# A selective-scan block with a gated feed-forward network: scan tiles of 8 states x 16 channels instead of 1 state x 128 channels

## What is computed

```
xz = x @ W_in.T;  x_ssm, z = split(xz)                     # 256 channels each
x_ssm = silu(causal_conv(x_ssm, conv_w, 4 taps) + conv_b)  # per channel, over time
proj = x_ssm @ W_x.T                                       # 16 columns B, 16 columns C, 1 for dt
dt = softplus(proj[..., -1:] * W_dt + b_dt)                # 256 channels
A = -exp(A_log)                                            # 256 channels x 16 states
h[t] = exp(dt[t] * A) * h[t-1] + (x_ssm[t] * dt[t]) * B[t] # 256 x 16 states, over 256 steps
y[t] = sum over states of h[t] * C[t]
out  = ((y + x_ssm * D) * silu(z)) @ W_out.T
```

## Time and profile before

| what | value |
|---|---|
| median of 3 runs | 1126.44 us |
| profiled execution | 1125.33 us |
| its span in the trace | 1123.5 us |
| instructions | 14735 |
| granted TensorE clock, mean | 0.969 of full |
| DMA traffic | 152.28 MB, mean 136 GB/s |
| VectorE idle before it starts the first U product | until 20.65 us |

### The profile page before, as it was taken

One profiled execution on the slowest core, in us unless ns is written; L12 is line 12 of the kernel. 1 busy time (PEld: TensorE's weight loads), 2 busy tenths in 40 slices (PEclk: granted clock), 3 DMA queues, 4 the chain that ended last, 5 costly groups with the idle time before them and its releaser, 6 DMA issues.

```text
span 1123.5 us, 14735 instructions
## 1 busy us (share of the span) xinstructions
PE 1028.0 (92%) x4928; PEld 649.0 (58%) x4928; DVE 1029.9 (92%) x1484; ACT 901.6 (80%) x1257; POOL 854.8 (76%) x499
## 2 busy tenths in 40 slices
PE   4656999999999999999999999999999999998997
PEld 1435566575756556565656657575665757555543
DVE  4999999999999999999999999999999999999511
ACT  7664988989798988979898898989889897987231
POOL 1677878878797888869788887978788797888540
PEclk8686999999999999999999999999999999999999
DMA  4762340705325070622507061340707043060000
GB/s 179 274 240 80 128 184 10 320 11 200 132 79 242 12 319 11 253 78 92 230 21 310 11 266 65 143 188 15 306 10 306 25 180 141 31 291 1 19 10 10
DMA packets 44060, 152.28 MB, mean 136 GB/s; under 512 B 4560, under 2 KB 24016, under 8 KB 27728
## 3 DMA queue, kind: packets, MB, share of 16 engines
q1 hardware_dynamic: 43600, 151.02, 34.1%
q10 hardware_dynamic: 384, 0.32, 0.1%
HBM read 146.08 MB, written 5.24 MB: 135 GB/s over the span
## 4 chain that ended last, share of the span: by engine, by line
PE 69%; ACT 16%; DVE 7%; issue 6%; POOL 2%; DMA 0%; ACTq 0%; DVEq 0%; POOLq 0%
PE G L705 33%; PE Y L690 14%; ACT dA L335 6%; PE G L727 4%; PE G L712 3%; ACT g L378 3%; DVE hb L598 3%; PE G L673 2%; PE Y L653 2%; PE Y L735 2%; PE G L657 2%; DVE U L591 2%; PE G L709 1%; ACT L351 1%; ACT xs L351 1%
## 5 line engine op out<-in xcount | busy, mean ns | idle before, releaser
L320 POOL TENSOR_TENSOR pb<-hb,cbc 128x1024 f32<-128x1024 f32 x256 | 602.9, 2363 | 179.9 <-DVE hb L598 139.6
L598 DVE TENSOR_TENSOR_SCAN hb<-dA,U 128x512 f32<-128x512 f32 x512 | 594.8, 1205 | 0.0
L335 ACT ACTIVATE dA<-dt,negA 128x510 f32<-128x510 f32 x512 | 342.2, 712 | 62.3 <-DVE hb L598 60.8
L591 DVE TENSOR_TENSOR U<-X,bbc 128x512 f32<-128x512 f32 x512 | 327.0, 686 | 7.2 <-ACT X L341 6.4
L690 PEld LDWEIGHTS Y<-ident,pb 128*128 128x128 f32 x2048 | 244.1, 145 | 111.0 <-issue 73.0
L690 PE MATMUL Y<-ident,pb 128*128 128x128 f32 x2048 | 272.1, 280 | 31.9 <-POOL pb L320 31.9
L705 PE MATMUL G<-hid,h_sb 128*128 128x512 f32 x512 | 232.6, 598 | 1.0 <-ACT g L494 0.8
L705 PE MATMUL G<-g,h_sb 128*128 128x512 f32 x512 | 229.8, 593 | 0.0
L705 PEld LDWEIGHTS G<-hid,h_sb 128*128 128x128 f32 x512 | 96.0, 193 | 110.5 <-issue 107.7
L705 PEld LDWEIGHTS G<-g,h_sb 128*128 128x128 f32 x512 | 92.6, 190 | 94.5 <-issue 90.3
L310 POOL TENSOR_TENSOR hid<-hid,g 128x512 f32<-128x512 f32 x64 | 80.1, 1273 | 7.8 <-ACT g L494 7.8
(11 more groups left out here) (91 smaller groups left out, 997.7 us busy)
## 6 DMA issues: line engine op xcount, KB each, us to landing
cbc<-scr SPq DMA_DIRECT2D x64, 1024.0 KB, 7.8
bbc<-scr SPq DMA_DIRECT2D x63, 1024.0 KB, 9.1
xT_sb<-xT_d SPq DMA_DIRECT2D x16, 256.0 KB, 2.7
xtok_sb<-xtok_d SPq DMA_DIRECT2D x16, 256.0 KB, 2.9
out_d<-r SPq DMA_DIRECT2D x16, 256.0 KB, 2.4
h_sb<-h_d SPq DMA_DIRECT2D x2, 1024.0 KB, 22.3
bbc<-scr SPq DMA_DIRECT2D x2, 512.0 KB, 4.6
scr<-rows SPq DMA_DIRECT2D x62, 16.0 KB, 1.5
```

The lines of the kernel that those rows point to most:

```text
L320: nc.gpsimd.tensor_tensor(pb[:, qs:qs + 2, :], hb[:, hs:hs + 2, :], cbc[:, n:n + 2, :], ALU.mult).then_inc(s_p, 1)
L335: nc.scalar.activation(halves(dA[:, u % DA_RING, :])[:, :, 1:SEQ], halves(dt[:, par, c, :])[:, :, 1:SEQ], ACT.Exp, scale=negA[:, c, n:n + ...
L591: nc.vector.tensor_tensor(U[i][:], X[:], bbc[:, n + i, :], ALU.mult).then_inc(s_u, 1)
L598: nc.vector.tensor_tensor_scan(hb[:, 2 * (v % H_PAIRS) + i, :], dA[:, u % DA_RING, :], U[i][:], 0.0, ALU.mult, ALU.add).then_inc(s_h, 1)
```

## The change

A tile becomes 8 states x 16 channels (partition 16 s + d). B and C, repeated 16 times, then serve all tiles with the same 8 states, and dt and dt*x have to be spread over the 8 states of a tile. What is done:

- dt and dt*x of a block are stored to DRAM (`store_steps`, 4 transfers of 256 KB a block) and read back so that each of 16 channels' rows goes to 8 partitions (`spread_steps`, 1 MB each, for 4 tiles; 8 a block), into 3 slots each. Each load serves two groups of 4 tiles, one for each half of the states.
- B and C are spread by 2 transfers of 256 KB each a block (`spread_B`, `spread_C`). ScalarE copies B, not dt*x, into the PSUM bank X, three times a block instead of twice.
- TensorE sums the states of 4 tiles with 4 products of 128 x 32 selecting weights, each at another 32-column position of the array, with 512 tokens moving (`sum_group`). The sum has channels on the partitions. It is begun by a product with diag(D). The turn, its copy and ScalarE's scaling by D go; z is made with channels on the partitions too.
- The convolution of channels 128 to 255 is four products with weights w_in * tap, accumulated at shifted tokens (`in_conv`); ScalarE copies the result (`copy_conv`). The other half stays on VectorE.
- Orders move: ScalarE's silu of the convolution to step 1 (with an activation table load more), the softplus to steps 7 and 8, one half after the other; the output projection to step 2; the second residual sum to step 6; GpSimd's sum of dt and product to steps 9, 11 and 12 and the second norm to 13; the start too.

The diff, cut to its core:

```diff
+SN, SD = 8, 16
+NG = NS // SN
+GT = 4
+GROUPS = NG * DI // SD // GT
+TILES = GROUPS * GT
+PARITIES = 2
+LOADS = NC * PARITIES
+SLOTS = 3
+def states_of(k):
+    return (0, 0, 1, 1, 1, 1, 0, 0)[k]
...
-        bbc = sb("bbc", [P, NS, TB])
-        cbc = sb("cbc", [P, NS, TB])
+        brep = sb("brep", [P, NG, TB])
+        crep = sb("crep", [P, 2, NG, TB])
+        dtr = sb("dtr", [P, SLOTS, GT, TB])
+        xdr = sb("xdr", [P, SLOTS, GT, TB])
...
+            def spread_B(b, g):
+                if b > 0:
+                    sp.wait_ge(s_X, 3 * b - g)
+                piece = scr_rows[b % 2, g * SN:(g + 1) * SN, :]
+                sp.dma_start(brep[:, g, :], piece.unsqueeze(1).to_broadcast([SN, SD, TB])).then_inc(s_b[g], 16)
+            def store_steps(b, c, scr, x, s_stored):
+                to = scr[b % 2, c].rearrange("e d q t -> q (e d) t")
+                sp.dma_start(to, x[:, c, :]).then_inc(s_stored[c], 16)
+            def spread_steps(b, c, e, scr, o, s_o):
+                slot = group_no(b, c, e) % SLOTS
+                piece = scr[b % 2, c, e].rearrange("d q t -> d (q t)")
+                sp.dma_start(flat(o[:, slot, :, :]), piece.unsqueeze(0).to_broadcast([SN, SD, GT * TB])).then_inc(s_o[slot], 16)
...
+                if scan and j > 0:
                     sp.wait_ge(s_u, TILES * j)
+                    spread_steps(j, 1, 0, scr_xd, xdr, s_xdr)
+                if scan:
+                    sp.wait_ge(s_dA, TILES * j + 3 * GT)
+                    spread_steps(j, 1, 1, scr_dt, dtr, s_dtr)
...
+                if scan:
+                    sp.wait_ge(s_u, TILES * j + 3 * GT)
+                    spread_steps(j, 1, 1, scr_xd, xdr, s_xdr)
+                if front:
+                    sp.wait_ge(s_rows, A + 1)
+                    store_rows(A, range(NT))
+                    sp.wait_ge(s_dt, 2 * A + 1)
+                    store_steps(A, 0, scr_dt, dts, s_dts)
+                    sp.wait_ge(s_xd, 2 * A + 1)
+                    store_steps(A, 0, scr_xd, xds, s_xds)
+                if front:
+                    sp.wait_ge(s_dts[0], 16 * (A + 1))
+                    sp.wait_ge(s_dA, TILES * j + 4 * GT)
+                    spread_steps(A, 0, 0, scr_dt, dtr, s_dtr)
+                    sp.wait_ge(s_dt, 2 * A + 2)
+                    store_steps(A, 1, scr_dt, dts, s_dts)
+                    sp.wait_ge(s_xds[0], 16 * (A + 1))
+                    sp.wait_ge(s_u, TILES * j + 4 * GT)
+                    spread_steps(A, 0, 0, scr_xd, xdr, s_xdr)
+                    sp.wait_ge(s_xd, 2 * A + 2)
+                    store_steps(A, 1, scr_xd, xds, s_xds)
+                    sp.wait_ge(s_store, 16 * NT * (A + 1))
+                    spread_B(A, 0)
+                    spread_C(A, (0,))
+                if front:
+                    sp.wait_ge(s_dA, TILES * j + 7 * GT)
+                    spread_steps(A, 0, 1, scr_dt, dtr, s_dtr)
+                    sp.wait_ge(s_u, TILES * j + 7 * GT)
+                    spread_steps(A, 0, 1, scr_xd, xdr, s_xdr)
+                    spread_B(A, 1)
+                    spread_C(A, (1,))
...
+            def fill_X(b, i):
+                g = i % 2
+                if i < 2:
+                    act.wait_ge(s_b[g], 16 * (b + 1))
+                if b > 0 or i > 0:
+                    act.wait_ge(s_u, TILES * b + (0, 2 * GT, 6 * GT)[i])
+                nc.scalar.activation(X[:], brep[:, g, :], ACT.Copy).then_inc(s_X, 1)
...
-                            nc.vector.tensor_tensor(U[i][:], X[:], bbc[:, n + i, :], ALU.mult).then_inc(s_u, 1)
+                            nc.vector.tensor_tensor(U[i][:], X[:], xdr[:, slot, q + i, :], ALU.mult).then_inc(s_u, 1)
...
+            def in_conv(b):
+                for s in range(TAPS):
+                    last = nc.tensor.matmul(halves(bank_c1(b))[:, :, s:SEQ], wc1[:, TAPS - 1 - s, :],
+                                            halves(xT_sb[:])[:, :, 0:SEQ - s], start=(s == 0), stop=(s == TAPS - 1),
+                                            skip_group_check=True)
+                last.then_inc(s_c1, 1)
...
+            def start_sum(b, c):
+                if b > 0:
+                    pe.wait_ge(s_gate, 2 * b - 1 + c)
+                pe.wait_ge(s_xs, 2 * b + 1 + c)
+                nc.tensor.matmul(Y[c][:], diagD[:, c, :], xs[:, b % 2, c, :], start=True, stop=False,
+                                 skip_group_check=True).then_inc(s_start, 1)
+            def sum_group(b, k):
+                c, e, _ = load_of(k)
+                pe.wait_ge(s_p, STEPS * b + 2 * k + 2)
+                for q in range(GT):
+                    rows32 = slice(q * 2 * SD, (q + 1) * 2 * SD)
+                    last = nc.tensor.matmul(Y[c][rows32, :], sel_sb[:, e, :], pb[:, (GT * k + q) % (2 * P_PAIRS), :],
+                                            start=False, stop=(k % (GROUPS // NC) == GROUPS // NC - 1),
+                                            skip_group_check=True, tile_position=(0, q * 2 * SD))
                 last.then_inc(s_y, 1)
```

More of the change, by code:

```diff
@@ L447, in _, with run @@
-            decay(0, 0, 1, True)
-            softplus_part(1, ACT.Relu)
-            decay(0, 0, 2, True)
-            decay(0, 0, 3, True)
-            times_D(0, 0, 0)
-            softplus_rest(1)
-            for u in range(4, AHEAD):
-                decay(0, 0, u, True)
-            def run(j, par, scan, intake, front, back, tail):
-                first = isinstance(j, int) and j == 0
+            for u in range(AHEAD):
+                decay(0, u)
+            def run(j, scan, intake, front, back, tail):
@@ L572, in _ @@
-            nc.vector.tensor_tensor(X[:], dt[:, 0, 0, :], xs[:, 0, 0, :], ALU.mult).then_inc(s_xdt, 1)
-            def run(j, par, scan, intake, front, back, tail):
-                first = isinstance(j, int) and j == 0
+            nc.vector.tensor_tensor(dts[:, 0, :], dts[:, 0, :], soft[:, 0, :], ALU.add).then_inc(s_dt, 1)
+            dve.wait_ge(s_dt, 1)
+            dve.wait_ge(s_xs, 2)
+            nc.vector.tensor_tensor(xds[:, 0, :], dts[:, 0, :], xs[:, 0, 0, :], ALU.mult).then_inc(s_xd, 1)
@@ L651, in _ @@
         def _(pe):
-            def in_proj(b, c):
-                nc.tensor.matmul(bank_in(b, c), win_sb[:, c * P:(c + 1) * P], xT_sb[:], start=True, stop=True).then_inc(s_ip, 1)
-            def z_proj(b, i):
-                for t in range(2):
-                    last = nc.tensor.matmul(BZ[i][:, t * DI:(t + 1) * DI], tile_of(xT_sb, 2 * i + t), win_sb[:, DI:2 * DI],
-                                            start=(t == 0), stop=True, skip_group_check=True)
-                last.then_inc(s_z, 1)
@@ L661, in rows_proj, with in_proj @@
-            def rows_proj(b, par):
-                for c in range(NC):
-                    pe.wait_ge(s_xs, 2 * b + 1 + c)
+            def in_proj(b):
+                nc.tensor.matmul(bank_in(b), win_sb[:, 0:P], xT_sb[:], start=True, stop=True).then_inc(s_ip, 1)
+            def in_conv(b):
[4 more added lines that the diff above has]
+                last.then_inc(s_c1, 1)
@@ L674, in dt_proj @@
                 last.then_inc(s_dtb, 1)
-            def start_sum(b, par, c):
-                if not (isinstance(b, int) and b == 0):
-                    pe.wait_ge(s_gy, 2 * b - 1 + c)
-                pe.wait_ge(s_xD, 2 * b + c + 1)
-                for t in range(NT):
-                    last = nc.tensor.matmul(Y[c][:, t, :], tile_of(xD[:], t), ident[:], is_transpose=True,
-                                            start=(t == 0), stop=False, skip_group_check=True)
-                last.then_inc(s_start, 1)
@@ L746, in _ @@
             pe.wait_ge(s_xT, 16)
-            for c in range(NC):
-                in_proj(0, c)
+            in_proj(0)
+            pe.wait_ge(s_wc1, 1)
+            in_conv(0)
+            pe.wait_ge(s_wx, 16)
+            rows_proj(0)
+            dt_proj(0)
+            pe.wait_ge(s_pre0, 4)
             z_proj(0, 0)
@@ L751, in _, with run @@
             z_proj(0, 1)
-            pe.wait_ge(s_wx, 16)
-            pe.wait_ge(s_tap, 6)
-            rows_proj(0, 0)
-            pe.wait_ge(s_zc, 2)
-            dt_proj(0, 0)
             pe.wait_ge(s_ident, 16)
-            def run(j, par, scan, intake, front, back, tail):
-                first = isinstance(j, int) and j == 0
+            pe.wait_ge(s_diag, NC)
+            pe.wait_ge(s_sel, 16)
+            def run(j, scan, intake, front, back, tail):
                 I, A, F, T = j + 2, j + 1, j - 1, j - 2
-                if isinstance(j, int) and j == 1:
+                if j == 1:
@@ L777, in run @@
-                    if v >= LAG and scan:
-                        sum_pair(j, v - LAG)
-                    if v == 0 and first:
-                        pe.wait_ge(s_xT, 16 * 2)
-                        in_proj(1, 0)
-                    if v == 0 and tail and not (isinstance(j, int) and j == NB):
+                    if v == 1 and back:
+                        sum_group(F, GROUPS - 1)
```

(14 more changed lines are left out.)

645 lines of the change are left out of this document (311 added, 334 removed).

## The result

The changed kernel takes **1490.3 us** (median of 4 runs, 1488.0 to 1500.1) beside 1125.9 us of the kernel before on the same chip: a ratio of 1.326, 95% interval 1.319 to 1.332. The forecast was 1093 us with a range of 1081 to 1150. The change made the kernel a third slower.

The account below looks back on a forecast made before the run. VectorE was taken to set the 64.60 us block, TensorE 1.5 behind: 1125.3 - 33.3 (taps) - 5.4 (residual wait) + 9 (start) - 6.5 (end) - 1.4 (turn, copy) = 1087.7, plus 4 for tight places and 1.1 to the median: 1093 us, range 1081 to 1150.

Parts of the forecast that it names:

- the DMA term: Block's loads and stores: 10 MB at 439 GB/s take 24 of 62 us, all hidden, so zero added.
- the case below: The exception to zero DMA cost: spreads running at half rate, 1173 us, chance 0.22.
- The first rival: Spreads and stores: 8 and 4 outermost get 8 and 4 engines, 4.8 us per MB, block 66.8, 1173 us; chance 0.22.
- G: TensorE: price of one group of 32-column products summing states, 1.0 us, eight groups a block; gain ends at 1.7.
- The third rival: TensorE: 32-column products do not overlap, 2.15 us a group, block 68.2, 1185 us, or 1329 wholly in line; chance 0.04.
- the pair: VectorE: two U products and two scans for a pair of tiles keep their shapes and stay at 3.42 us.
- the residual sum: VectorE: its 8.9 us wait in 14 places for the output projection goes; 3.49 belongs to the end, so -5.4.
- the second rival: Loads in time, engines late (X fills, gate, TensorE's loop): 1 to 2 us a block, 1108 to 1123 us; chance 0.20.
- The second X fill: ScalarE: must end between the U products of step 3 and step 4; fits with 0.8 us to spare.
- the gate behind step 9: A block's first gate, 38.8 us in, needs a TensorE group that ends at 38.2: 0.6 us to spare.
- The start: Before the first U: dt and dt*x go out and come back, first U at 29.8 instead of 20.65; taken as +9.
- VectorE sets the block and TensorE is 1.5 us behind it: Steady block of 64.60 us: VectorE, idle only 0.36 us, bounds it; cutting one engine alone is worth little.

Follow-up runs that it names:

- experiment 2: Changed kernel with partitions renumbered channel by channel (8 x channel + state), each dt and dt*x spread as two transfers of 8 channels: 1356.5 us.
- experiment 7: The kernel before, each 1 MB broadcast issued as 8 transfers to 16 neighbouring partitions each, one row still read: 1232.3 us.
- experiment 8: Changed kernel, dt and dt*x spreads reading one row for all 128 partitions, which leaves out the right channels: 1187.9 us.
- experiment 9: Changed kernel, partitions channel by channel, stores in four parts, the spreads' 16 source rows 64 bytes apart instead of 8 KB: 1139.7 us.
- experiment 3: Changed kernel, its partition order kept, each dt and dt*x spread issued as 8 transfers to 16 neighbouring partitions each: 1553.9 us.
- experiment 11: Changed kernel, partitions channel by channel, four-part stores, early x load, spreads in 512 KB halves, one dt half before a store: 1115.0 us, 0.991 of the kernel before.
- Experiment 12: The kernel before with only the convolution of the upper 128 channels moved to TensorE, from the second block on: 1165.3 us, ratio 1.035.
- experiment 1: Changed kernel with partitions renumbered to 8 x channel + state, so every spread of dt, dt*x, B and C has 16 outermost: 1218.1 us, ratio 1.081.

## Why the prediction was wrong, step by step

**The step that failed** is the DMA term: "At full rate the engines move 439 GB/s", "With 1 MB in 2.4 us ... hidden. Bounds: zero, and the case below." The rate was carried over from a row of a transfer with 128 on both sides to ones with 8 and 4 outermost, and the wait that follows was put at zero. Measured, 1.05 MB take 7.8 us in the stretch that VectorE waits for (135 GB/s) and 8.7 us in its slow windows (120 GB/s), over three times as long. VectorE stands for 24.5 us a block on loads; after the first U its waits for X and dt*x come to 366 us, and the first U itself is 17 us later than forecast. That is 383 of the 397 us between 1093 and 1490.

**The first rival had the mechanism and half of the price.** It named the outermost counts, 8 and 4, and the traces show that they set the number of busy engines: shares of 0.26 while only stores move, about 0.5 with 8 outermost, about 1 with 16. The Trainium skill (DMA: Bandwidth & Descriptors, on why a DMA increments its semaphore by 16) has this rule, and the traces agree with it. But the rival gave 4.8 us per MB, each engine at its full speed, and so 66.8 us a block and 1173. The second factor was in no bound of mine: in the slow windows each of the 8 engines moves 104 to 127 GB/s / 8 = 13 to 16 GB/s, where one of the 16 of before moves 439/16 = 27. It is no constant, as up to 210 GB/s at the same share in the changed kernel and up to 214 in experiment 2 show. Experiments 7, 8 and 9 point to the side that is written: the flat pattern gives 409, the 16 x 8 pattern mostly 205 to 256 with near or far source rows, 16 neighbours at a time 197 with one row read. But the side that is read is not cleared: the same 16 neighbours with 16 rows read gave 131 (experiment 3).

The Trainium skill (SBUF — State Buffer, Door 1: The DMA port swizzle) says that partitions share 16 ports for DMA by three bits and one bit of their number, and (DMA: Bandwidth & Descriptors, The descriptor swizzle) that a flat transfer to 128 partitions gives each engine a port of its own. My estimate from those two pages, if the engines walk their parts in step: 8 engines on partitions 16 apart write 4 ports at a time, a quarter of 436 or 109 GB/s (measured 104 to 127, but up to 210 in other stretches); 16 engines on partitions 8 apart write 8 ports, 218 (measured mostly 205 to 256); 16 neighbours are 4 ports, 109 (measured 131 in experiment 3, but 197 in experiment 7); 8 engines on partitions 8 apart are 4 ports, 109 (measured 127 to 214 in experiment 2). So the slow stretches fit and the fast ones do not, unless the engines are out of step there. Neither ports nor the step of the engines were observed, so this reading is argued, not shown, and the cause of the second factor stays open.

**The range and the chances.** The range's upper end, 1150, held only the mild half of the first rival; no row bounded the speed of one engine in the new pattern from below. With every transfer of the rival twice as long, its own line comes to some 31 us a block and over 1500 (an estimate). Slower had 0.24 and should have had more, as a stated rule spoke for it and nothing in the trace against it but the absence of a row.

**The terms that held**, read in the changed kernel itself:
- A sum group: four 32-column products (8 passes) show 1.07 us, and the next group starts 1.00 later; predicted G = 1.0. The third rival is out.

```profile
607.95 1.07 PE L752 MATMUL Y<-pb,sel_sb 128*32 128x512 f32 x8
608.95 3.70 PE L761 MATMUL G<-g,h_sb 128*128 128x512 f32 x8
```

- VectorE: the pair at 3.44 (predicted 3.42), busy time 31.9 us less (predicted 33.3), no wait at the residual sum, as predicted; 61.9 us busy in the block measured above (predicted 62.0). With the transfers mended, experiment 11 lands at 1115.
- The 1115 lies inside the second rival's 1108 to 1123, but not for its reason: there the loads were in time. The block is 63.4 us against the forecast's 62.0, and the 0.61 and 1.06 us are the first X fill of two blocks in a row, which waits for B's spread (39.4 us in all). The second X fill and the gate behind step 9, which the prediction called tight, show no wait in the block from 606.88 to 670.28.
- The start: predicted first U at 29.8; measured 47.09 in the changed kernel. The 29.29 of experiment 11 is near it by luck: it waits for 512 KB pieces, and at another rate than the sum assumed.

**One reading was wrong and did not show in the time.** "VectorE sets the block and TensorE is 1.5 us behind it" reads the idleness of VectorE alone. Experiment 12 shows that TensorE could not take 2.6 us more, although VectorE got 2.2 us less to do: TensorE, busy for 97% of the window, was a bound, and the gap between it and VectorE's 99% was not slack. Whether VectorE was a bound as well isn't shown, as no run relieves TensorE alone.

## What to carry to other kernels

Before a transfer is changed in shape, write down for both of its sides what is outermost and which partitions the engines write at the same moment, and take a rate only from a transfer with the same pattern; the busy share alone does not tell the rate. Before work is moved to an engine that is idle for 3% of the time, look at the chain of work that ended last: if it is mostly that engine's, the idle time is not room. If a rule speaks for a slow case and no row speaks against it, forecast that case, with a price in which every factor that no row bounds is slow. And where a buffer is exchanged through a slow queue, cut the exchange in halves before reordering the queue: that gave 2.3% here (with one half moved ahead of a store), where of two reorderings of whole transfers one cost 0.8% and the other gave nothing.

## What was not expected of the hardware

- A queue with all 16 engines busy moves some 131, 197, 205 to 256 or 410 to 439 GB/s, depending on the pattern of partitions and rows (experiments 3, 7, 1, 8 and the kernel before).
- With 8 engines busy it moves some 100 to 210 GB/s in the changed kernel and 127 to 214 in experiment 2, within one and the same kernel.
- An issue of a 1 MB transfer holds SP for 0.6 us while the queue keeps up and for up to 14.61 us in the block above when it is behind (17.9 at most over the span); all of SP's later waits and small transfers queue behind that.
- Small loads suffer as much as big ones: the load of x, 256 KB, lands in 15.9 us in the changed kernel, in 2.7 before, in 5.2 in experiment 11.
